# A four-part graph network on one core: another order of ScalarE's stages in the fourth gated pass, and a last part with four row buffers

## The chip, the cores and the metric

The kernel runs on one core of a Trainium2 chip. The metric is the device time of one execution in microseconds (us). The engines are TensorE (PE; its weight loads are PEld), VectorE (DVE), ScalarE (ACT), GpSimd (POOL) and SyncE (SP); an engine name with a q, as ACTq, is its queue of instructions that are not computation.

## The reference, cut to what matters

12,500 nodes with 64 features, 200,000 edges sorted by destination. Four networks follow each other, each with a layer norm and a relu ahead and its result added to `x`:

```
h = relu(layernorm(x)); x += GIN(h)            # sum over edges of relu(h[src]), then a two-layer MLP
h = relu(layernorm(x)); x += gated(h)          # 4 steps: message by edge type, sum over edges, GRU cell
h = relu(layernorm(x)); x += gcn(h)            # 2 convolutions: degree-normalised sum over edges
h = relu(layernorm(x)); x += edge_network(h)

GRU cell:  r, z = sigmoid(...);  n = tanh(i_n + r * h_n);  feat = (1 - z) * n + z * feat
edge net:  h = [x_dst, x_src - x_dst] @ W.T + b          # per edge
           h = (h - mean(h)) / sqrt(var(h) + eps) * gamma + beta    # over all edges
           h = where(h >= 0, h, 0.3 * h)
           result = segment_sum(h, dst) / max(counts, 1)
```

## The kernel before, in words

Edges lie in 1563 rows of 128 edges, nodes in 98 blocks of 128. A pass over the edges handles 1660 visits of (row, block) in 166 groups of ten, two groups to a span, 83 spans. There are eight passes: GIN, three gated ones, `MIXED` (the fourth gated pass with the first work of the convolutions), `CONV`, `LAST` and `EDGE`. In a pass:

- POOL gathers every row's 128 source nodes from a table in DRAM (line 476), one indirect DMA for a row, into a ring `RINGF` of 300 rows. For row 300 and on it waits until SP has told it (`ring_free`, L367) that PE is done with the rows that are overwritten. It can't begin a pass before the table of that pass is whole: SP counts the writes of the table (`sent`) and then raises `table_ready`.
- DVE writes one-hot matrices `OH` from the destinations (L1027), PE multiplies them with the gathered rows (L683) into PSUM, after two matmuls of zeros that clear the places (L679), and DVE adds the places to the sums in `A` (L1052).
- The node work runs beside this in steps called positions, 132 to a pass (`SLOTS`), each on a chunk of two blocks. The function `positions` emits, for each engine, the stages (lag, stage) in the order written: at position p a stage with lag k works on chunk number p - k. The first 83 positions go with the spans; the other 49 follow when all groups are summed. A table of chunks by position is worked out at run time; where no chunk is complete yet, a position works on a spare one, and so the passes always run all 132. A pass's table is whole in the first few positions behind the spans; the rest are spare ones, and PE and DVE begin the next pass only behind them.

In `MIXED` a chunk goes through these stages: DVE `pick` (L1084, lag 0), PE turns it, ACT `copied` (L540, 0), PE `gates`, ACT `gates` = Sigmoid (L570, 1), DVE `pre` (L1130, L1133, 1), ACT `bent` = Tanh (L576, 1), DVE `mix_last` (L1140 to L1166, 2) with `centre` (L1094, L1096), ACT `root` = two Squares with sums (L561) and a Sqrt (L564), lag 3, DVE `scaled` (reciprocal L1103, L1112, 3), PE `turn2` (L733), ACT `copied2` (L548, 3), PE, DVE `convolved` (L1177, L1178, 4), ACT `send` (L596, 4), which writes the table. ACT also fetches `XIN` for the chunk (L583). Sqrt is in another activation table than Sigmoid and Tanh, and the compiler puts an `ACT_TABLE_LOAD` ahead of each change.

The last part follows the `EDGE` pass, in which the rows before the norm were written to `kept` in DRAM; the one-hot matrices lie in DRAM as bf16 (`shorts`). For each of 166 groups: SP loads the rows (`LOADED`, two buffers, L430) and the one-hots (`OH16`, four buffers, L404, which waits for the product four groups back); DVE subtracts a middle (L1339) and takes max(0.3 t, t) (L1344, `ACTED`, four buffers); POOL splits that in two steps (`split` L507, `low` L502, one group later) into three bf16 parts; PE clears ten places (`zero`, L679) and runs 30 matmuls (L683); DVE adds them to the sums (L1331, `edge_add` of the group four back, between L1339 and L1344). `groups_in_fours` emits groups 0 to 5 and then a loop of four groups. Behind the loop, DVE writes a weight for each node and feature (L1349), multiplies and adds in two halves (L1359, L1360), and SP writes each half out (L437).

Of the kernel before, what the change touches and what calls it, by code (L numbers as in the profile page):

```python
# [13 lines left out]
P = 128  # L14
# [54 lines left out]
def gnn_kernel(nc, x, dst_rows, src_cols, type_cols, row_ends, batch_ends, L0_W1, L0_b1, L0_W2, L0_b2, L1_Wt, L1_b,  # L69
# [15 lines left out]
    with ExitStack() as ctx:  # L85
# [107 lines left out]
        LOADED, MOVED = (cut(RINGF, k * 2 * GRP * D, [2, GRP, D]) for k in range(2))  # L193
        ACTED, REST = (cut(RINGF, (1 + k) * 4 * GRP * D, [HOLD, GRP, D]) for k in range(2))
# [7 lines left out]
        def bank(k):  # L202
# [46 lines left out]
        kept_out, kept_in, drow_in = (sems(f"{n}0", f"{n}1") for n in ("kept_out", "kept_in", "drow_in"))  # L249
        short_out, short_in = sems("short_out0", "short_out1"), sems(*(f"short_in{k}" for k in range(HOLD)))  # L250
# [6 lines left out]
            sem(f"e_{n}") for n in ("moved", "acted", "rest", "low", "product", "added"))  # L257
        result, stored = sems("result", "stored")
# [66 lines left out]
        def _(sp):  # L325
# [90 lines left out]
            for h in range(2):  # L416
                sp.wait_ge(kept_out[h], 16)
                sp.dma_start(LOADED[:, h, :, :], kept[:, h * GRP:(h + 1) * GRP, :]).then_inc(kept_in[h], 16)
            for h in range(2):
                sp.wait_ge(kept_out[h], SPAN * 16)  # L420
            sp.wait_ge(e_counted, GROUPS)
# [17 lines left out]
            sp.wait_ge(stored, 32)  # L439
# [76 lines left out]
        def _(act):  # L516
# [40 lines left out]
            def root(turn):  # L557
# [840 lines left out]
```

## Time and profile before

| what | value |
|---|---|
| median of 3 runs | 16602.79 us (16602.6 to 16603.92) |
| the profiled execution, its own time | 16601.05 us |
| its span in the trace | 16599.2 us |
| granted PE clock, mean | 0.523 |
| busy: PE, PEld | 67%, 54% |
| busy: DVE, ACT, POOL | 34%, 14%, 74% |

Times in the trace count from the start of the span. A row of the timeline gives start and duration in us, the engine, the line of the kernel, the operation, what it writes <- reads, how many are merged, and in brackets how long the engine sat idle before it and what ended that. POOL's busy time is the issue of its gathers. "issue" is time in which the engine waited for nothing that the profile shows. POOL holds the largest share of the chain that ended last; the order in which engines are busy says where in the 16.6 ms other engines hold it up.

### The profile page before, as it was taken

The numbers are of one execution on the slowest core, as the hardware profiler recorded it, in microseconds if no ns is written. First come the engines' busy times: TensorE is split into PE (matmuls) and PEld (weight loads), VectorE is DVE, ScalarE is ACT, GpSimd is POOL, SyncE is SP. The second block draws the span as 40 slices with busy tenths as digits, with TensorE's granted clock in tenths as the row PEclk, the third lists the DMA queues.
The fourth block names the chain that finished last, engine by engine and source line by source line (L and its number), as shares of the span: only waits on it lengthen the run. The fifth ranks groups of instructions, "written<-read, shape, count | busy, mean of one in ns | idle before, by whom it ended". The sixth has DMA issues, their size and how long they took to land.

```text
span 16599.2 us, 246663 instructions
## 1 busy us (share of the span) xinstructions
PE 11186.9 (67%) x47842; PEld 8971.1 (54%) x47843; DVE 5583.8 (34%) x12782; ACT 2283.6 (14%) x5885; POOL 12248.7 (74%) x12861
## 2 busy tenths in 40 slices
PE   4666787767776677766776665666565555787776
PEld 3455555555555555555565553455454444687765
DVE  3222333323332243322443333322232223422247
ACT  1111130001100020000222224211100000100000
POOL 6777677776777767777677776677777777777776
PEclk5555555556655565555755555555555555555555
DMA  2111121112211121111211111222211111333345
GB/s 53 40 40 41 43 67 40 39 38 50 51 39 38 38 61 40 39 38 38 62 33 32 32 32 36 57 66 65 59 39 32 32 32 34 86 93 83 83 136 191
DMA packets 727921, 891.48 MB, mean 54 GB/s; under 512 B 251262, under 2 KB 352847, under 8 KB 727200
## 3 DMA queue, kind: packets, MB, share of 16 engines
q0 software_dynamic: 400544, 411.38, 14.2%
q1 hardware_dynamic: 113184, 233.19, 4.4%
q10 hardware_dynamic: 213984, 244.81, 4.2%
q14 instruction: 161, 1.32, 0.0%
q8 instruction: 48, 0.79, 0.0%
HBM read 590.99 MB, written 297.44 MB: 54 GB/s over the span
## 4 chain that ended last, share of the span: by engine, by line
POOL 51%; issue 23%; DMA 14%; PE 6%; DVE 2%; DVEq 1%; SPq 1%; ACT 0%; ACTq 0%; POOLq 0%
POOL RINGF L476 51%; DMA RINGF<-tab_gated,IDX 7%; PE ps L683 4%; DMA RINGF<-tab_gcn,IDX 4%; DMA RINGF<-tab_gin,IDX 2%; DMA RINGF<-tab_edge,IDX 1%; PE ps L679 1%; DVEq L1067 1%; SPq L365 1%; PE ps L777 0%; DVE TEMP L1084 0%; DVE ps L1140 0%; DVE TEMP L1142 0%; PE ps L716 0%; DVE TEMP L1130 0%
## 5 line engine op out<-in xcount | busy, mean ns | idle before, releaser
L476 POOL DMA_INDIRECT RINGF<-tab_gated,IDX x6252 | 5903.9, 944 | 2044.5 <-issue 1775.8
L683 PEld LDWEIGHTS ps<-RINGF,OH 128*128 128x128 f32 (+1 forms) x28220 | 5316.4, 296 | 1739.6 <-issue 1739.6
L683 PE MATMUL ps<-RINGF,OH 128*128 (+1 forms) x28220 | 5560.3, 392 | 1026.3 <-SPq L362 1022.0
L476 POOL DMA_INDIRECT RINGF<-tab_gcn,IDX x3126 | 2951.0, 944 | 1098.5 <-issue 943.4
L1052 DVE TENSOR_TENSOR A<-A,ps 128x640 f32 x1162 | 954.4, 821 | 7886.6 <-PE ps L683 7886.6
L679 PE MATMUL ps<-ZERO 1*128 1x325 bf16 x2656 | 927.8, 451 | 2460.7 <-issue 2454.1
L476 POOL DMA_INDIRECT RINGF<-tab_gin,IDX x1563 | 1483.4, 949 | 504.0 <-issue 444.0
L476 POOL DMA_INDIRECT RINGF<-tab_edge,IDX x1563 | 1476.4, 945 | 506.5 <-issue 446.4
L1027 DVE TENSOR_TENSOR OH<-ps,DLOC 128x1280 f32<-128x1280 f32 x1162 | 1723.4, 1484 | 0.3
L679 PEld LDWEIGHTS ps<-ZERO 1*128 1x128 bf16 x2656 | 174.5, 99 | 2818.0 <-issue 2812.6
L733 PE MATMUL ps<-IDENT,TEMP 128*64 128x128 f32 x1848 | 535.9, 390 | 619.4 <-DVE TEMP L1112 202.7
L821 PE MATMUL ps<-IDX,OH 128*128 (+1 forms) x3320 | 727.6, 351 | 304.5 <-ACT OH L640 304.5
L764 PE MATMUL ps<-WG,TEMP 128*128 128x256 f32 x2112 | 902.4, 575 | 0.0
L777 PE MATMUL ps<-WT,TEMP 65*128 65x256 f32 x2112 | 887.0, 565 | 15.5 <-ACT TEMP L548 15.2
L821 PEld LDWEIGHTS ps<-IDX,OH 128*128 128x128 f32 x3320 | 724.7, 332 | 316.3 <-issue 316.3
L570 ACT ACTIVATE TEMP<-ps 128x256 f32<-128x256 f32 x528 | 201.1, 381 | 4865.5 <-PE ps L764 4864.7
L716 PE MATMUL ps<-IDENT,TEMP 128*128 128x128 f32 (+1 forms) x1320 | 387.1, 391 | 649.7 <-DVE TEMP L1084 608.8
L548 ACT ACTIVATE TEMP<-ps 64x256 f32<-64x256 f32 x924 | 346.3, 375 | 3378.0 <-PE ps L733 3039.9
L811 PE MATMUL ps<-A,TEMP 128*128 x3320 | 748.1, 423 | 8.0 <-DVE TEMP L1252 8.0
L716 PEld LDWEIGHTS ps<-IDENT,TEMP 128*128 128x128 f32 (+1 forms) x1320 | 167.3, 177 | 1066.3 <-issue 1064.0
L811 PEld LDWEIGHTS ps<-A,TEMP 128*128 128x128 f32 x3320 | 728.0, 333 | 8.9 <-issue 8.9
L764 PEld LDWEIGHTS ps<-WG,TEMP 128*128 128x128 f32 x2112 | 633.2, 300 | 118.9
(206 smaller groups left out, 7972.5 us busy)
## 6 DMA issues: line engine op xcount, KB each, us to landing
tab_gated<-TEMP ACTq DMA_DIRECT2D x528, 256.0 KB
RINGF<-tab_gated,IDX POOLq DMA_INDIRECT x6252
shorts<-TEMP ACTq DMA_DIRECT2D x166, 320.0 KB
TEMP<-dloc_dram SPq DMA_DIRECT2D x166, 320.0 KB
kept<-OH SPq DMA_DIRECT2D x166, 320.0 KB
RINGF<-kept SPq DMA_DIRECT2D x166, 320.0 KB, 3.3
OH<-shorts SPq DMA_DIRECT2D x166, 320.0 KB, 3.0
RINGF<-tab_gcn,IDX POOLq DMA_INDIRECT x3126
```

What stands on the lines that cost most here:

```text
L476: nc.gpsimd.indirect_dma_start(out=RINGF[:, at:at + D], out_offset=None, in_=table, in_offset=bass.IndirectOffsetOnAxis(ap=index[:, k:k + ...
L548: nc.scalar.activation(XT[0:D, odd, :], ps_t2[0:D, :], func).then_inc(s_copied2, 1)
L679: nc.tensor.matmul(ps[:, base + k * BANK:base + k * BANK + HALF * PITCH], ZERO[:, 0:P], ZERO[:, 0:HALF * PITCH], start=True, stop=True)
L683: return nc.tensor.matmul(ps[:, base:][:, bass.ds(place, width)], onehots_, rows_, start=False, stop=False, skip_group_check=True)
L716: ins = nc.tensor.transpose(ps_t[0:width, k * P:(k + 1) * P], PICK[:, odd, k, 0:width], IDENT[:, :])
L733: ins = nc.tensor.transpose(ps_t2[0:D, k * P:(k + 1) * P], NEXT[:, odd, k, :], IDENT[:, :])
L764: ins = nc.tensor.matmul(ps_gate[odd][:, k, :], XG[:, odd, k * P:(k + 1) * P], WG[:, :], start=False, stop=False, skip_group_check=True)
L777: ins = nc.tensor.matmul(out_[:, k, :], XT[0:rows, odd, k * P:(k + 1) * P], weights, start=True, stop=True)
L811: ins = nc.tensor.matmul(ps_u[:, h, u // HALF, u % HALF, :], OTS[:, h, u, :], Af[:, D:][:, bass.ds(at[u], D)], start=True, stop=True)
L821: ins = nc.tensor.matmul(ps_stat[w][:, bass.ds(2 * g, 2)], table[:, h, u:u + 2, :].rearrange("p u f -> p (u f)"), MASK[:, bass.ds(g * GRP ...
L1027: return V.tensor_tensor(OH[:, h, :, :], ps_ramp[h].unsqueeze(1).broadcast_to([P, GRP, P]), cols.unsqueeze(2).broadcast_to([P, GRP, P]), A ...
L1052: ins = V.tensor_tensor(into, into, ps_g[:, h, :, :, 0:D], ALU.add)
```

## The change: what it does

In `MIXED`, ACT's stage `root` is cut in two, `spread` (the Squares) and `root` (the Sqrt). They ran first in a position, at lag three; now `spread` stands behind `copied` and `root` behind `bent`, both at lag two. On DVE `scaled` now comes ahead of `pick`. In GIN and `LAST` the two halves follow each other as before.

In the last part `LOADED` has four buffers in place of two (`MOVED`, with two, lies elsewhere), four groups are loaded ahead, and SP issues a row load when the group four back has been moved. ACT writes the zeros of each group's places into PSUM, from the constant `NONE`, when the group two back has been added, and PE's two matmuls of zeros are gone: PE waits for ACT's zeros in their place. ACT also writes the weights, one instruction for each of 98 blocks, between the zeros; DVE's one instruction for them is gone. The result is finished and written in four pieces of 42, 32, 18 and 6 blocks.

```diff
--- before.py
+++ after.py
@@
+PIECES = [(0, 42), (42, 74), (74, 92), (92, 98)]
@@
-        LOADED, MOVED = (cut(RINGF, k * 2 * GRP * D, [2, GRP, D]) for k in range(2))
-        ACTED, REST = (cut(RINGF, (1 + k) * 4 * GRP * D, [HOLD, GRP, D]) for k in range(2))
+        LOADED, ACTED, REST = (cut(RINGF, k * HOLD * GRP * D, [HOLD, GRP, D]) for k in range(3))
+        MOVED = cut(RINGF, 14 * GRP * D + NB * D, [2, GRP, D])
@@ block.sync
-            for h in range(2):
-                sp.wait_ge(kept_out[h], 16)
-                sp.dma_start(LOADED[:, h, :, :], kept[:, h * GRP:(h + 1) * GRP, :]).then_inc(kept_in[h], 16)
+            def load_back(g, k):
+                sp.dma_start(LOADED[:, k, :, :], kept[:, bass.ds(g * GRP, GRP), :]).then_inc(kept_in[k], 16)
+
+            def load_group(g, h, k, i, q):
+                if later(g, HOLD):
+                    sp.wait_ge(e_moved, g - HOLD + 1)
+                    load_back(g, k)
+                    sp.wait_ge(e_product, g - HOLD + 1)
+                    load_short(g, k)
+
+            for g in range(HOLD):
+                sp.wait_ge(kept_out[g % 2], (g // 2 + 1) * 16)
+                load_back(g, g)
...
-            def load_group(g, h, k, i, q):
-                if later(g, 2):
-                    sp.wait_ge(e_moved, g - 1)
-                    sp.dma_start(LOADED[:, h, :, :], kept[:, bass.ds(g * GRP, GRP), :]).then_inc(kept_in[h], 16)
-                if later(g, HOLD):
-                    sp.wait_ge(e_product, g - HOLD + 1)
-                    load_short(g, k)
             groups_in_fours(load_group)(sp)
-            for k in range(2):
+            for k, (first, last) in enumerate(PIECES):
                 sp.wait_ge(result, k + 1)
-                sp.dma_start(out[:, k * NB // 2:(k + 1) * NB // 2, :], X3[:, k * NB // 2:(k + 1) * NB // 2, :]
-                             ).then_inc(stored, 16)
+                sp.dma_start(out[:, first:last, :], X3[:, first:last, :]).then_inc(stored, 16)
@@ block.scalar
-            def root(turn):
+            def spread(turn):
                 def stage(s, odd, i, tail):
                     act.wait_ge(s_cen, turn * SLOTS + s + 1)
                     for k in range(CH):
                         nc.scalar.activation(SQ[:, k, :], CEN[:, odd, k, :], ACT.Square, scale=0.125,
                                              accum_out=LN[:, odd, 1, k:k + 1]).then_inc(s_sq, 1)
+                return stage
+
+            def root(turn):
+                def stage(s, odd, i, tail):
                     act.wait_ge(s_sq, (turn * SLOTS + s + 1) * CH)
@@ block.scalar, the mixed pass
-            positions(act, no_groups, (3, root(1)), (1, gates(MIXED)), (0, copied(MIXED, P)),
-                      (1, bent(MIXED)), (3, copied2(MIXED, ACT.Copy)), (0, fetch),
+            positions(act, no_groups, (1, gates(MIXED)), (0, copied(MIXED, P)), (2, spread(1)),
+                      (1, bent(MIXED)), (2, root(1)), (3, copied2(MIXED, ACT.Copy)), (0, fetch),
                       (4, send(MIXED, tab_gcn[0], D, s_conv, 0)))
@@ block.scalar, the last part
+            act.wait_ge(e_moved, 1)
+
+            def weigh(b):
+                nc.scalar.activation(A3[:, bass.ds(b, 1), D:P], ST[:, S_SCALE:S_SCALE + 1, :], ACT.Copy,
+                                     scale=CNT[:, bass.ds(b, 1)]).then_inc(e_weighed, 1)
+
+            def zero_places(g, h, k, i, q):
+                if later(g, 2):
+                    act.wait_ge(e_added, g)
+                nc.scalar.activation(places[:, h, :, 0:HALF * PITCH], NONE[:, :, 0:1].broadcast_to([P, 2, HALF * PITCH]),
+                                     ACT.Copy).then_inc(e_zeroed, 1)
+                if isinstance(g, int):
+                    for b in range(3 * g, 3 * g + 3):
+                        weigh(b)
+                elif h == 0:
+                    weigh(i + 15)
+            groups_in_fours(zero_places)(act)
@@ block.tensor, sum_group
-                if later(g, 2):
-                    pe.wait_ge(e_added, g)
-                    pe.sem_inc(pe_go, 1)
-                zero(base)
+                pe.wait_ge(e_zeroed, g + 1)
+                pe.sem_inc(pe_go, 1)
                 pe.wait_ge(e_low, g + 1)
@@ block.vector, the mixed pass
-            positions(dve, sum_edges(MIXED), (0, pick(MIXED, False)), (3, scaled(MIXED, 1, False)), (2, mix_last),
+            positions(dve, sum_edges(MIXED), (3, scaled(MIXED, 1, False)), (0, pick(MIXED, False)), (2, mix_last),
                       (1, pre(MIXED)), (4, convolved(MIXED, 0, 4)))
@@ block.vector, sum_step and after it
-                    dve.wait_ge(kept_in[h], i * 16 + 16)
-                    V.tensor_tensor(MOVED[:, h, :, :], LOADED[:, h, :, :], middle, ALU.subtract).then_inc(e_moved, 1)
+                    dve.wait_ge(kept_in[k], q * 16 + 16)
+                    V.tensor_tensor(MOVED[:, h, :, :], LOADED[:, k, :, :], middle, ALU.subtract).then_inc(e_moved, 1)
...
-            link(V.tensor_tensor(FEAT, ST[:, S_SCALE:S_SCALE + 1, :].broadcast_to([P, NB, D]), over_f(CNT), ALU.mult))
...
+            dve.sem_inc(dve_go, 1)
+            dve.wait_ge(e_weighed, NB)
-            for k in range(2):
-                half = slice(k * NB // 2, (k + 1) * NB // 2)
+            for first, last in PIECES:
+                part = slice(first, last)
```

ACT's instructions in one position of `MIXED` behind the spans, before (L561 Squares, L564 Sqrt, L570 Sigmoid, L540 `copied`, L576 Tanh, L548 `copied2`):

```order
L561 ACTIVATE TEMP<-TEMP 128x64 x2
L564 ACT_TABLE_LOAD
L564 ACTIVATE TEMP<-TEMP,EPSC 128x2
L570 ACT_TABLE_LOAD
L570 ACTIVATE TEMP<-ps 128x256
L540 COPY TEMP<-ps 128x256
L576 ACTIVATE ps<-TEMP 128x2x64
L548 ACTIVATE TEMP<-ps 64x256
```

And now (L579 Sigmoid, L545 `copied`, L566 Squares, L585 Tanh, L573 Sqrt, L553 `copied2`):

```order
L579 ACT_TABLE_LOAD
L579 ACTIVATE TEMP<-ps 128x256
L545 COPY TEMP<-ps 128x256
L566 ACTIVATE TEMP<-TEMP 128x64 x2
L585 ACTIVATE ps<-TEMP 128x2x64
L573 ACT_TABLE_LOAD
L573 ACTIVATE TEMP<-TEMP,EPSC 128x2
L553 ACTIVATE TEMP<-ps 64x256
```

The Squares and the Sqrt with its table load moved from the head of the position to both sides of the Tanh; there are two table loads in either. DVE's instructions at the head of such a position, before (L1084 `pick`, L1103 and L1112 `scaled`, L1140 the first of `mix_last`; L1067 reads a chunk's number):

```order
L1084 COPY TEMP<-A 128x256
L1103 RECIPROCAL TEMP<-TEMP 128x2
L1112 SCALAR_TENSOR_TENSOR TEMP<-TEMP 128x128
L1067 ISA
L1067 TENSOR_LOAD LISTS
L1067 ISA x2
L1140 ISA
L1140 TENSOR_TENSOR ps<-A,ps 128x2x64
```

And now (L1127 and L1136 `scaled`, L1108 `pick`, L1091 reads the chunk's number; `mix_last` follows):

```order
L1127 RECIPROCAL TEMP<-TEMP 128x2
L1136 SCALAR_TENSOR_TENSOR TEMP<-TEMP 128x128
L1091 ISA
L1091 TENSOR_LOAD LISTS
L1091 ISA x2
L1103 REGISTER_ALU
L1105 REGISTER_ALU
L1108 ISA
L1108 COPY TEMP<-A 128x256
```

`pick`, with the reading of its chunk number, moved from ahead of the reciprocal to a place behind `scaled`. PE's instructions in the last part's loop, from the last reading of the places to a group's first matmuls, before:

```order
L671 TENSOR_LOAD LISTS
L847 ISA
L679 MATMUL ps<-ZERO 128x325 x2
L853 REGISTER_ALU
L683 ISA
L683 MATMUL ps<-RINGF,OH 128x64 x3
```

And now:

```order
L697 ISA
L697 TENSOR_LOAD LISTS
L875 REGISTER_ALU
L709 ISA
L709 MATMUL ps<-RINGF,OH 128x64 x3
```

The two matmuls of zeros left, and nothing came in their place but a wait.

## Rows read from the trace of the kernel before

**Rows 1.** The page, part 4: the chain that ended last, by engine.

```profile
POOL 51%; issue 23%; DMA 14%; PE 6%; DVE 2%; DVEq 1%; SPq 1%; ACT 0%; ACTq 0%; POOLq 0%
```

**Rows 2.** Timeline of POOL: start, duration (us), engine, line, operation [idle before].

```profile
10039.54 0.94 POOL L476 DMA_INDIRECT RINGF<-tab_gcn,IDX  x1 [65.45 <-issue]
...
10476.97 0.94 POOL L476 DMA_INDIRECT RINGF<-tab_gcn,IDX  x1 [62.21 <-SPq L367]
```

**Rows 3.** Timeline of ACT and DVE, one position after the mixed pass's last group.

```profile
10206.74 0.29 ACT L564 ACTIVATE TEMP<-TEMP,EPSC 128x2 f32<-128x2 f32 x1
10207.05 1.28 ACT L570 ACT_TABLE_LOAD   x1
10207.06 0.17 DVE L1103 RECIPROCAL TEMP<-TEMP 128x2 f32<-128x2 f32 x1 [2.39 <-ACT TEMP L564]
...
10211.31 0.29 DVE L1133 TENSOR_TENSOR TEMP<-TEMP,ps 128x128 f32<-128x128 f32 x1
10211.63 0.28 ACT L576 ACTIVATE ps<-TEMP 128x128 f32<-128x128 f32 x1 [2.63 <-DVE TEMP L1133]
10211.84 0.36 ACT L548 ACTIVATE TEMP<-ps 64x256 f32<-64x256 f32 x1
...
10213.82 0.29 DVE L1084 COPY TEMP<-A 128x256 f32 x1 [0.75 <-issue]
...
10214.85 1.28 ACT L564 ACT_TABLE_LOAD   x1
```

**Rows 4.** Line L564 in two stretches (min/median/max ns, first and last start); timeline.

```profile
L564 ACT ACTIVATE TEMP<-TEMP,EPSC x21: 295/296/296, 8403.8 to 8789.7; 128x2 f32<-128x2 f32 x21
...
L564 ACT ACTIVATE TEMP<-TEMP,EPSC x52: 295/295/296, 9992.3 to 10464.1; 128x2 f32<-128x2 f32 x52
...
10036.15 0.36 ACTq L596 DMA_DIRECT2D tab_gcn<-TEMP  x1
...
10440.06 0.29 ACT L564 ACTIVATE TEMP<-TEMP,EPSC 128x2 f32<-128x2 f32 x1
...
10470.86 1.27 ACT L628 ACTIVATE TEMP<-OH 128x1280 bf16<-128x1280 f32 x1 [4.22 <-DVE OH L1027]
```

**Rows 5.** Chain in order of time, last part: start, us, what.

```profile
16300.92 0.70 PE ps L679 x2
16301.62 1.71 PE ps L683 x30
```

**Rows 6.** Timeline of POOL and DVE in the last part's loop.

```profile
16038.67 1.25 POOL L507 TENSOR_TENSOR RINGF<-RINGF 128x640 f32<-128x640 f32 x1
...
16041.68 1.25 POOL L507 TENSOR_TENSOR RINGF<-RINGF 128x640 f32<-128x640 f32 x1
...
16300.23 1.25 POOL L507 TENSOR_TENSOR RINGF<-RINGF 128x640 f32<-128x640 f32 x1 [0.76 <-DVE RINGF L1344]
...
16301.43 1.25 POOL L502 TENSOR_TENSOR RINGF<-RINGF 128x640 bf16<-128x640 f32 x1
...
16302.31 1.06 DVE L1344 SCALAR_TENSOR_TENSOR RINGF<-RINGF 128x640 f32<-128x640 f32 x1
16303.45 1.25 POOL L507 TENSOR_TENSOR RINGF<-RINGF 128x640 f32<-128x640 f32 x1 [0.76 <-DVE RINGF L1344]
...
16304.15 0.82 DVE L1339 TENSOR_TENSOR RINGF<-RINGF,ps 128x640 f32<-128x640 f32 x1 [0.79 <-DMA RINGF<-kept]
```

**Rows 7.** Timeline of the end; last row: the page's part 6.

```profile
16566.47 1.25 POOL L507 TENSOR_TENSOR RINGF<-RINGF 128x640 f32<-128x640 f32 x1 [0.76 <-DVE RINGF L1344]
...
16570.49 6.68 DVE L1349 TENSOR_TENSOR A<-ST,CNT 128x6272 f32<-128x6272 f32 x1
...
16578.07 1.78 DVE L1331 TENSOR_TENSOR A<-A,ps 128x640 f32 x2 [0.90 <-DVE A L1349]
...
16590.25 3.42 DVE L1360 TENSOR_TENSOR RINGF<-RINGF,A 128x3136 f32<-128x3136 f32 x1
...
RINGF<-kept SPq DMA_DIRECT2D x166, 320.0 KB, 3.3
```

More of the change, by code:

```diff
@@ L59 @@
 TINY = 1e-20
+PIECES = [(0, 42), (42, 74), (74, 92), (92, 98)]
 FAR = 1 << 20
 assert (GROUPS - 6) % HOLD == 0
+assert PIECES[-1][1] == NB == 3 * 6 + 2 * ((GROUPS - 6) // HOLD)
 assert GROUPS * GRP == VISITS and 2 * SPAN == GROUPS and SPAN % 2 == 1 and SLOTS % 2 == 0
@@ L247, in gnn_kernel @@
         x3_in, x_held = sems("x3_in", "x_held")
-        kept_out, kept_in, drow_in = (sems(f"{n}0", f"{n}1") for n in ("kept_out", "kept_in", "drow_in"))
-        short_out, short_in = sems("short_out0", "short_out1"), sems(*(f"short_in{k}" for k in range(HOLD)))
+        kept_out, short_out, drow_in = (sems(f"{n}0", f"{n}1") for n in ("kept_out", "short_out", "drow_in"))
+        kept_in, short_in = (sems(*(f"{n}{k}" for k in range(HOLD))) for n in ("kept_in", "short_in"))
         short_set = sem("short_set")
@@ L257, in gnn_kernel @@
             sem(f"e_{n}") for n in ("moved", "acted", "rest", "low", "product", "added"))
+        e_zeroed, e_weighed = sems("e_zeroed", "e_weighed")
         result, stored = sems("result", "stored")
@@ L414, in _ @@
                 keep(GROUPS - 2 + h, h)
-            for h in range(2):
-                sp.wait_ge(kept_out[h], 16)
-                sp.dma_start(LOADED[:, h, :, :], kept[:, h * GRP:(h + 1) * GRP, :]).then_inc(kept_in[h], 16)
+            def load_back(g, k):
[9 more added lines that the diff above has]
+                load_back(g, g)
+            sp.wait_ge(e_counted, GROUPS)
             for h in range(2):
                 sp.wait_ge(kept_out[h], SPAN * 16)
-            sp.wait_ge(e_counted, GROUPS)
             for g in range(HOLD):
@@ L609, in _ @@
             positions(act, no_groups, (1, hidden), (0, copied(GIN, D)), (4, typed(GIN)),
-                      (4, send(GIN, tab_gated[1], TYPES * D, s_typed, GIN)), (3, copied2(GIN, ACT.Copy)), (2, root(0)),
-                      (2, store(x_gin, 0)))
+                      (4, send(GIN, tab_gated[1], TYPES * D, s_typed, GIN)), (3, copied2(GIN, ACT.Copy)), (2, spread(0)),
+                      (2, root(0)), (2, store(x_gin, 0)))
             act.wait_ge(sums, SUMS_AT[1])
@@ L633, in _ @@
             positions(act, shorten, (0, copied2(CONV, ACT.Relu)), (1, send(CONV, tab_gcn[1], D, s_conv, 1)))
-            positions(act, no_groups, (1, copied2(LAST, ACT.Copy)), (0, root(2)), (0, store(x_last, 2)),
+            positions(act, no_groups, (1, copied2(LAST, ACT.Copy)), (0, spread(2)), (0, root(2)), (0, store(x_last, 2)),
                       (2, send(LAST, tab_edge, D, s_conv, 2)))
@@ L1356, in _ @@
             dve.wait_ge(x3_in, 16)
-            for k in range(2):
-                half = slice(k * NB // 2, (k + 1) * NB // 2)
-                link(V.tensor_tensor(SUMS[:, half, :], SUMS[:, half, :], FEAT[:, half, :], ALU.mult))
-                V.tensor_tensor(X3[:, half, :], X3[:, half, :], SUMS[:, half, :], ALU.add).then_inc(result, 1)
+            dve.sem_inc(dve_go, 1)
+            dve.wait_ge(e_weighed, NB)
+            for first, last in PIECES:
+                part = slice(first, last)
+                link(V.tensor_tensor(SUMS[:, part, :], SUMS[:, part, :], FEAT[:, part, :], ALU.mult))
+                V.tensor_tensor(X3[:, part, :], X3[:, part, :], SUMS[:, part, :], ALU.add).then_inc(result, 1)
 def kernel(**inputs):
```

2 lines of the change are left out of this document (1 added, 1 removed).

## The prediction

> **What bounds the kernel now.** I first read the chain that ended last [rows 1]. POOL leads it with 51%, and the next share, "issue", is mostly the handover between its gathers: over the whole program POOL is the pacer, and another engine costs time only where POOL stands still or where there is no gathering. So I went through POOL's timeline for its long pauses. Between the fourth gated pass and the first convolution there are two [rows 2]: 65.45 us before the first gather of `CONV`, in which the table must become whole, and 62.21 us before its 301st. That the second one is released by SP's L367 (`ring_free`) says that the ring was full: PE had not begun `CONV`. It couldn't, since it was still in the spare positions of `MIXED`. The 300 gathers before it took 10414.76 - 10039.54 = 375.2 us (10414.76 is where the pause began), 1.25 us each.
>
> Next, one such position in the timeline of ACT and DVE [rows 3]. It is a circle. The Sqrt ends at 10207.03 and lets DVE's reciprocal go, which had waited 2.39; DVE runs through `scaled`, `mix_last` and `pre` and ends L1133 at 10211.60; the Tanh had waited for it for 2.63; then ACT has `copied2`, the two DMAs, the Squares, a table load from 10214.85 and the next Sqrt. Each engine waits once for the other. From 9992.3 to 10440.06 that makes 48 positions [rows 4], 9.33 us each.
>
> Last I read the last part, where nothing is gathered. Its chain in order of time is PE alone: 0.70 of zeros, 1.71 of products [rows 5], and the reading of the next places. POOL's L507 starts at 16041.68 for group 5 and at 16566.47 for group 165 [rows 6, 7]: 3.28 us per group.
>
> **The circle in `MIXED`.** Now the Sqrt follows the Tanh directly, so the DMAs and the Squares no longer lie on the way from DVE's `pre` to the Sqrt. Counted from a Sqrt's end: DVE's old stretch to the end of L1133, 10211.60 - 10207.03 = 4.57; `pick` now lies in it, 0.75 of idle before it and 0.29 itself [rows 3], 1.04; Tanh 0.28, table load 1.28, Sqrt 0.29, handovers 0.07. Sum 7.53 us. The same way of counting gives for before 4.57 + 0.03 + 3.22 (Tanh's start to the load's) + 1.28 + 0.31 = 9.41 against the 9.33 measured, so it errs by under 0.1. Neither engine's own work is longer: ACT's is 9.33 - 2.63 = 6.7 us, DVE's from the reciprocal at 10207.06 to the end of `pick` at 10214.11 is 7.05. PE's matmuls for a position lie beside the circle. The Squares wait for `centre`, behind which DVE still has a copy and `pre`'s two operations of 0.29 [rows 3]; two Squares of 64 elements lie beside those. I take 7.53, 1.80 less per position; the bounds are DVE's 7.05 and the old 9.33.
>
> What that gives. (1) The last chunk that the table needs is picked in the first position behind the spans and sent four positions later, by the DMA at 10036.15 [rows 4]. That is 4 x 1.80 = 7.2 less; but its `pick` now stands behind `scaled`, which costs about 1.1 once. 6.1 us. (2) From POOL's first `CONV` gather to the release of its ring it took 437.4 us, with 44 positions in them: 44 x 1.80 = 79 less is 358, and POOL needs 375 to fill the ring. The pause goes whole, 62.2 - 0.3 = 61.9 us. It would come back if a position took over 7.92. What is late next is POOL's own issue of gathers. Both together: 68.0 us. While the spans run, a longer or shorter position costs nothing: POOL covers it (see the slower rival). The other passes have the same instructions as before.
>
> **The last part's loop.** Taking the zeros from PE shortens its 3.28 by at least 0.6, to 2.7 or less. So PE is out, and I ask who is next. The rows on POOL and DVE [rows 6] show it: L1344, which has the same size as L1339 (0.82 us), took 1.06 when it began at 16302.31, while L502 ran until 16302.68, and POOL's next L507 started only when it was done, after 0.76 of idle. So the three work in turn: L507 1.21 to L502's start, L502 1.25, then 0.76, together 3.22 us for a group (16300.23 to 16303.45). That turn has no PE and no DMA in it. I take 3.22: 160 groups x 0.06 = 9.6 us. The row loads had DVE wait 0.79 before L1339 once here; SP still issues each behind the one-hot load that waits for PE's product, so the four buffers alone don't start it earlier, but PE's earlier product does, and with its wait gone DVE still meets POOL's L502 on the way. Below, the bound is groups 4 and 5, 16038.67 to 16041.68, 3.01 us, when DVE was ahead and L1344 slipped in between POOL's two; above, the old 3.28.
>
> By the Trainium skill (SBUF — State Buffer, "SBUF: two separate sides") VectorE with two SBUF inputs and GpSimd share one port pair by an exclusive lock that is held for the whole instruction. This case's rows agree: 1.06 in place of 0.82 where they overlap. Without such a lock the loop would fall to DVE's three operations of 0.82 and their handovers, about 2.85, and the part would gain 70 us more or less; with it hardly anything is left for the two matmuls to give.
>
> ScalarE's write of zeros, 2 x 325 per partition into PSUM, isn't in the trace. Nearest rows: Tanh with 128 into PSUM, 0.28 [rows 3]; a copy of 1280, 1.27 [rows 4]. I take 0.8, between them by size. It starts when DVE has added the group two back, and that add ends before L1344, so even at 1.27 the zeros are there about 0.7 us after POOL's `low`; a product of 1.7 that starts that much later still ends a group ahead of its add. It costs nothing at either end. The 98 weights of 64 elements each (0.28 or less) go where ACT waits for DVE.
>
> **The end.** Before, POOL's last L507 began at 16566.47 and DVE's last add ended at 16579.85 [rows 7], 13.4 us: PE was two groups behind, and DVE's 6.68 us for the weights stood in the way. Now: L507 and two L502 3.7, of which the last product waits; PE takes 1.71 for each product and 3.28 - 0.70 - 1.71 = 0.87 between them, so two products from the first L502's end (2.6 after L507's start) end at 6.9; add 1.1. That is 8.0, 5.4 less. The final four operations become eight: same elements, 4 x 0.16 of fixed cost more (6.68 against 2 x 3.42 gives 0.16), 0.6 us. Behind the last one at 16593.67 lay 5.5 us until the span's end, for a half of 1568 KB; the last piece has 192 KB, and 320 KB land in 3.3 [rows 7]; with the third piece's rest I take 3.5. 2.0 - 0.6 = 1.4 us.
>
> **Sum.** 6.1 + 61.9 + 9.6 + 5.4 + 1.4 = 84.4 us. The profiled execution took 16601.05 (span 16599.2), so 16516.7 in its frame; the median of the runs is 1.7 above it, so 16518.4.
>
> **Rivals.**
> A. The loop finds the faster turn of 3.01 and keeps it: 160 x 0.21 = 34 us more, 16485. For: there are no waits on row loads at first. Against: a row load must be issued two groups after the product that lets SP go on, and it takes 3.3 us; before, the faster turn held for four groups only.
> B. A switch of tables costs more behind the Tanh than the load's 1.28. If ACT first had to run empty, for about as long as one more load, a position would take 8.81, 0.52 less in place of 1.80: 1.0 us ahead of the table, 23 of the pause. With the last part 40 us, 16562. Against: the load at 10207.05 starts 0.02 after the end of the Sqrt ahead of it [rows 3], so nothing is paid there. The Trainium skill (ScalarE: Activation LUTs, "What ACT_TABLE_LOAD costs") has such a drain, ~1380 ns, with each switch, by which the sum would be 16567; the row agrees with its 1283 ns for the load and shows no drain.
> C. The pause is only handed on: POOL fills the ring at once, but DVE and PE in `CONV`, which also wait for ACT's shortening of the one-hots (1.27 each), can't follow, and the 62 us come back at the pass's end: 16580. Against: PE starts `CONV` with fewer rows waiting than before, when the ring was full, and POOL made no third long pause.
> D. Slower. The stages of a position in `MIXED` also run between PE's groups. PE takes its queue in order: `turn` waits for `pick`, which now waits behind `scaled` for the previous position's Sqrt. If that stretches a span over POOL's 1563 x 1.25 / 83 = 23.5 us, each microsecond costs 83. At 25 us: 124 lost against 84 won, 16643. Against: when PE was catching up, positions followed each other every 19.3 us [rows 4], and `scaled`'s Sqrt is then a whole span old. It decides from 24.6 us.
>
> **How the numbers follow.** The forecast 0.73, A 0.10, B 0.06, C 0.06, D 0.05. The forecast's own range is 16495 (a position of 7.05 and half of A) to 16545 (a position of 8.4: 21 us of the pause stay, and 3.5 ahead of the table). A change within 0.2%, 33 us, counts as none; a measurement of this kernel tells hardly less. A and B are faster by more than that; C lies within; D is slower: 0.89, 0.06, 0.05. The range of 8 in 10 takes in A and goes up to the forecast's end and a part of B: 16482 to 16558.
>
> **What would show it.** In the changed kernel's trace: no pause of POOL before the 301st gather of `CONV`, and about 59 us before its first; the Sqrt every 7.5 us behind `MIXED`'s spans, with the load 0.02 behind the Tanh; in the last part L507 every 3.2 us, with 0.76 of idle after L1344, L1344 over 0.82, no L679; the weights' instruction gone; less than 9 us from the last L507 to the last add. A pause at the 301st gather, or a position over 7.92, would make the large term wrong; L507 every 3.0 us would be A; positions over 23.5 us apart in the spans, D.

## The result, and the profile after

The changed kernel takes 16527.74 us (median of 6 runs, 16527.18 to 16529.08), beside 16602.53 for the kernel before (6 runs, 16600.69 to 16603.92). That is 74.8 us less, a ratio of 0.9955 with a 95% interval of 0.9942 to 0.9968. 16518.4 had been forecast, 84.4 less. Sign and range hold, and so does the large term in `MIXED`. The term for the last part's loop does not. On one of the chips used for the experiments most runs had each pass some 4 us longer (the kernel before: 16633 in place of 16602), so each experiment is compared with the kernel before on its own chip, and by stretches of the trace.

The time by stages, from POOL's gathers in both traces (us):

| stretch | before | after | forecast |
|---|---|---|---|
| last gather of `MIXED` to first of `CONV` | 65.45 | 59.16 | 59.35 |
| first gather of `CONV` to its last | 2013.68 | 1951.54 | 1951.8 |
| last gather of all to the span's end | 592.76 | 587.15 | 576.4 |
| everything else (two spans less the above) | 13927.3 | 13927.5 | as before |

The chain that ended last, by engine (the page, part 4), answers to [rows 1]:

```profile
POOL 58%; issue 23%; DMA 15%; PE 1%; DVE 1%; SPq 1%; DVEq 0%; POOLq 0%; ACTq 0%; ACT 0%
```

PE's share fell from 6% to 1% and POOL's rose by 7 points. That is no gain of 5% of the span: the chain in the last part merely runs over POOL now where it ran over PE, and the next rows show how little that part's time changed. What a chain names is whose work it passed through, not what would be saved.

POOL's timeline at `CONV`'s beginning, answering to [rows 2]:

```profile
10033.05 0.94 POOL L481 DMA_INDIRECT RINGF<-tab_gcn,IDX  x1 [59.16 <-issue]
...
10449.54 0.94 POOL L481 DMA_INDIRECT RINGF<-tab_gcn,IDX  x1 [0.90 <-issue]
```

The pause of 62.21 is gone. The only idle time over 0.6 us that POOL has left in `CONV` is 0.90 before the 334th gather.

One position behind `MIXED`'s spans, in the timeline of ACT and DVE, answering to [rows 3]:

```profile
10199.67 0.29 DVE L1157 TENSOR_TENSOR TEMP<-TEMP,ps 128x128 f32<-128x128 f32 x1
10199.99 0.28 ACT L585 ACTIVATE ps<-TEMP 128x128 f32<-128x128 f32 x1 [0.30 <-DVE TEMP L1157]
10200.29 1.28 ACT L573 ACT_TABLE_LOAD   x1
...
10201.59 0.29 ACT L573 ACTIVATE TEMP<-TEMP,EPSC 128x2 f32<-128x2 f32 x1
...
10201.91 0.17 DVE L1127 RECIPROCAL TEMP<-TEMP 128x2 f32<-128x2 f32 x1 [0.48 <-ACT TEMP L573]
...
10203.54 0.45 DVE L1108 COPY TEMP<-A 128x256 f32 x1 [0.91 <-issue]
...
10207.36 0.28 ACT L585 ACTIVATE ps<-TEMP 128x128 f32<-128x128 f32 x1 [0.30 <-DVE TEMP L1157]
```

The Tanh, the table load 0.02 behind its end, the Sqrt 0.02 behind the load: nothing is paid for a drain. DVE's wait for the Sqrt fell from 2.39 to 0.48, the Tanh's wait for DVE from 2.63 to 0.30. The line's own summary for the stretch, answering to [rows 4]:

```profile
L573 ACT ACTIVATE TEMP<-TEMP,EPSC x52: 295/295/296, 9991.5 to 10369.5; 128x2 f32<-128x2 f32 x52
```

51 steps in 378.0 us are 7.41 us for each, where [rows 4] give (10464.1 - 9992.3) / 51 = 9.25.

The last loop turn of the last part, PE, POOL, DVE and ACT, answering to [rows 5, 6]; the number in brackets is the idle time ahead:

```profile
16485.82 1.78 PE L709 MATMUL ps<-RINGF,OH 128*128 128x64 bf16 x30 [1.28 <-issue]
...
16489.07 1.82 PE L709 MATMUL ps<-RINGF,OH 128*128 128x64 bf16 x30 [1.47 <-issue]
...
16492.15 1.78 PE L709 MATMUL ps<-RINGF,OH 128*128 128x64 bf16 x30 [1.25 <-issue]
...
16494.42 1.25 POOL L512 TENSOR_TENSOR RINGF<-RINGF 128x640 f32<-128x640 f32 x1 [0.76 <-DVE RINGF L1368]
16494.85 0.82 DVE L1363 TENSOR_TENSOR RINGF<-RINGF,ps 128x640 f32<-128x640 f32 x1 [0.51 <-DMA RINGF<-kept]
...
16495.81 1.79 PE L709 MATMUL ps<-RINGF,OH 128*128 128x64 bf16 x30 [1.89 <-issue]
...
16496.73 0.71 ACT L668 ACTIVATE ps<-NONE 128x650 f32<-128x650 f32 x1 [2.23 <-DVE A L1355]
...
16498.94 1.81 PE L709 MATMUL ps<-RINGF,OH 128*128 128x64 bf16 x30 [1.33 <-issue]
```

PE has 1.8 of products for each group and stands idle for the rest, but the releaser is "issue": no other engine holds it. Four starts on are 16498.94 - 16485.82 = 13.12 us, 3.28 each, exactly what a group took before. What PE's own queue does in such a gap is in the trace too (`--source L697`, the reading of the ten places, from 16496.9 to 16498.9):

```profile
L697 PEldq TENSOR_LOAD <-LISTS x3: 327/332/334, 16497.1 to 16498.1; - x3
```

Three reads of 0.33 us, half a microsecond apart. The first starts when the products of the group before still run, the last ends at 16498.4, and behind it come the group's waits and register operations until its first product at 16498.94. Ahead of the reads the queue has a register operation for each of the ten places, spread over the products. So it is at work from one group's first product to the next one's.

The end, answering to [rows 7]:

```profile
16497.64 1.25 POOL L512 TENSOR_TENSOR RINGF<-RINGF 128x640 f32<-128x640 f32 x1 [0.76 <-DVE RINGF L1368]
...
16505.32 1.80 PE L709 MATMUL ps<-RINGF,OH 128*128 128x64 bf16 x30 [1.32 <-issue]
16507.38 0.82 DVE L1355 TENSOR_TENSOR A<-A,ps 128x640 f32 x1 [2.30 <-PE ps L709]
16508.46 2.96 DVE L1384 TENSOR_TENSOR A<-A 128x2688 f32<-128x2688 f32 x1 [0.26 <-DVE A L1355]
...
16514.44 8.59 SPq L443 DMA_DIRECT2D out<-RINGF  x4
...
16522.10 0.56 DVE L1385 TENSOR_TENSOR RINGF<-RINGF,A 128x384 f32<-128x384 f32 x1
```

POOL's last `split` to the last add's end: 10.56 us (13.38 before). From there to the span's end: 17.1 (19.3 before).

### The profile page after: what moved, and what is told of

Same layout as the page of the kernel before. It is cut to its first block, busy times and chain, and to the rows that moved or that the text cites. A ratio compares the mean times of both kernels' runs of the same rounds, so it can differ in the third digit from the quotient of the medians.

```text
span 16525.3 us, 246610 instructions
## 1 busy us (share of the span) xinstructions
PE 11107.3 (67%) x47510; PEld 8984.8 (54%) x47511; DVE 5602.7 (34%) x12785; ACT 2430.0 (15%) x6149; POOL 12247.7 (74%) x12861
## 3 DMA queue, kind: packets, MB, share of 16 engines
q14 instruction: 162, 1.33, 0.0%
## 4 chain that ended last, share of the span: by engine, by line
POOL 58%; issue 23%; DMA 15%; PE 1%; DVE 1%; SPq 1%; DVEq 0%; POOLq 0%; ACTq 0%; ACT 0%
POOL RINGF L481 56%; DMA RINGF<-tab_gated,IDX 8%; DMA RINGF<-tab_gcn,IDX 4%; DMA RINGF<-tab_gin,IDX 2%; DMA RINGF<-tab_edge,IDX 2%; POOL RINGF L507 1%; PE ps L709 1%; POOL RINGF L512 1%; SPq L368 0%; DVEq L1091 0%; PE ps L803 0%; DMA tab_gin<-A 0%; POOLq L472 0%; PE ps L705 0%; PE ps L742 0%
## 5 line engine op out<-in xcount | busy, mean ns | idle before, releaser
L705 PE MATMUL ps<-ZERO 1*128 1x325 bf16 x2324 | 811.6, 450 | 2313.6 <-issue 2308.2
L579 ACT ACTIVATE TEMP<-ps 128x256 f32<-128x256 f32 x528 | 201.0, 381 | 4970.7 <-PE ps L790 4969.6
L803 PE MATMUL ps<-WT,TEMP 65*128 65x256 f32 x2112 | 920.2, 583 | 15.4 <-ACT TEMP L553 15.3
L553 ACT ACTIVATE TEMP<-ps 64x256 f32<-64x256 f32 x924 | 346.2, 375 | 3403.2 <-PE ps L759 3064.1
```

Source lines behind the costliest of these rows:

```text
L553: nc.scalar.activation(XT[0:D, odd, :], ps_t2[0:D, :], func).then_inc(s_copied2, 1)
L705: nc.tensor.matmul(ps[:, base + k * BANK:base + k * BANK + HALF * PITCH], ZERO[:, 0:P], ZERO[:, 0:HALF * PITCH], start=True, stop=True)
L803: ins = nc.tensor.matmul(out_[:, k, :], XT[0:rows, odd, k * P:(k + 1) * P], weights, start=True, stop=True)
```

## The experiments

Three questions: which part of the change brought what; why the last part's loop kept its 3.28; what would shorten it. All edits are to the changed kernel. "Last part" is from POOL's last gather to the span's end, and a group's time is from POOL's split for the sixth group to the last one, over 160.

**1. The last part's edits alone.** `MIXED` in the order of before.

```
-  positions(act, ..., (1, gates(MIXED)), (0, copied(MIXED, P)), (2, spread(1)), (1, bent(MIXED)), (2, root(1)), ...
+  positions(act, ..., (3, spread(1)), (3, root(1)), (1, gates(MIXED)), (0, copied(MIXED, P)), (1, bent(MIXED)), ...
-  positions(dve, ..., (3, scaled(MIXED, 1, False)), (0, pick(MIXED, False)), (2, mix_last), ...
+  positions(dve, ..., (0, pick(MIXED, False)), (3, scaled(MIXED, 1, False)), (2, mix_last), ...
```

> Only the last part is changed; ScalarE's and VectorE's order in the mixed pass is that of before. By the two traces the last part gave 5.6 us (592.8 to 587.2 us from POOL's last gather to the end), so the main theory (two separate effects that add) expects 16597 us, a ratio of 0.9997, with POOL's pause of 62 us at the 301st gather of CONV there again. Rival: the pause and the last part are coupled by the state in which the passes run; then it is below 16590 us.

Measured: 16602.28 us beside 16607.65 for the kernel before on the same chip, ratio 0.9997 (0.9987 to 1.0007). The pause is back:

```profile
10477.48 0.94 POOL L481 DMA_INDIRECT RINGF<-tab_gcn,IDX  x1 [62.56 <-SPq L370]
```

The last part takes 587.66, as with the whole change (587.15), beside 592.76. So all that the last part's edits bring is 5.1 us by the traces and 5.4 by the medians, whose interval doesn't exclude nothing at all; `MIXED`'s orders bring the rest.

**2. ACT's new order alone**, DVE's `pick` ahead of `scaled` as before.

```
-  positions(dve, ..., (3, scaled(MIXED, 1, False)), (0, pick(MIXED, False)), (2, mix_last), ...
+  positions(dve, ..., (0, pick(MIXED, False)), (3, scaled(MIXED, 1, False)), (2, mix_last), ...
```

> The changed kernel, but VectorE keeps its old order, pick ahead of scaled; ScalarE's new order stays. Theory 'circle': pick then lies outside the way from Sqrt to Tanh, where it is short by 7.4 - 1.04 = 6.3 us, and a position is bound by VectorE's own 7.05 us or ScalarE's 6.7: Sqrts 7.0 to 7.2 us apart behind the spans, no pause at the 301st gather, the gap before CONV's first gather 57 us in place of 59.2, the time 1 to 3 us below the changed kernel's 16527.7. Rival 'VectorE's swap is needed': with pick first, the reciprocal comes late and positions stay near 9 us, so that 30 to 60 us of the pause come back.

Measured: 16527.31 us, 80.3 less than before on that chip (the whole change: 74.8 on its own), ratio 0.9952 (0.9935 to 0.9968). The line of the Sqrt, and POOL's first gather of `CONV`:

```profile
L573 ACT ACTIVATE TEMP<-TEMP,EPSC x52: 295/295/296, 9993.1 to 10340.2; 128x2 f32<-128x2 f32 x52
```

```profile
10030.72 0.94 POOL L481 DMA_INDIRECT RINGF<-tab_gcn,IDX  x1 [52.93 <-issue]
```

A position takes 347.1 / 51 = 6.81 us and the gap 52.93, 6.2 less than with both orders; 57 had been expected, and 7.0 to 7.2 for a position. DVE's half of the change is a loss. With both orders the first `pick` behind the spans, at 9993.28, stands 19.4 us behind `MIXED`'s last gather, since it has to wait for `scaled`; here, as in the kernel before, it stands 15.5 behind it. That is 3.9 once. The four positions behind it take 2.9 less, since `pick` no longer lies between the Sqrt and the next Tanh, and 0.6 are lost from the fourth `pick` after it to the last send.

**3. DVE's new order alone**, ACT's as before.

```
-  positions(act, ..., (1, gates(MIXED)), (0, copied(MIXED, P)), (2, spread(1)), (1, bent(MIXED)), (2, root(1)), ...
+  positions(act, ..., (3, spread(1)), (3, root(1)), (1, gates(MIXED)), (0, copied(MIXED, P)), (1, bent(MIXED)), ...
```

> The changed kernel, but ScalarE keeps its old order in the mixed pass (Squares and Sqrt first, lag three), and VectorE has the new one, pick behind scaled. Theory 'circle': pick is added to a way that was 9.33 us long, so 10.4 us for a position, the pause at the 301st gather 62 + 44 x 1.04 = 108 us, the gap before CONV about 70 us, in all 16597 + 51 = 16648 us. Rival 'VectorE's order alone gives part of the gain': the position is below 9.33 us and the time below 16597.

Measured: 16657.34 us (one run), 50 more than the kernel before.

```profile
10537.40 0.94 POOL L481 DMA_INDIRECT RINGF<-tab_gcn,IDX  x1 [115.69 <-SPq L370]
```

The gap ahead of `CONV` is 73.21, a position (10524.5 - 9993.8) / 51 = 10.41. The circle that the forecast drew, with one link longer, gives a longer pause: the same mechanism with the other sign.

**4. The zeros back on PE**, none by ACT.

```
-                if later(g, 2):
-                    act.wait_ge(e_added, g)
-                nc.scalar.activation(places[:, h, :, 0:HALF * PITCH], NONE[:, :, 0:1].broadcast_to([P, 2, HALF * PITCH]),
-                                     ACT.Copy).then_inc(e_zeroed, 1)
...
-                pe.wait_ge(e_zeroed, g + 1)
-                pe.sem_inc(pe_go, 1)
+                if later(g, 2):
+                    pe.wait_ge(e_added, g)
+                    pe.sem_inc(pe_go, 1)
+                zero(base)
```

> The changed kernel with PE's two matmuls of zeros back in the last part's loop, and none of ScalarE's zeros. Theory 'PE's instruction stream' (the time between two groups' products is that in which PE's queue reads the ten places into registers, and the zeros lay beside it): the loop stays at 3.27 us per group and the time within 2 us of 16527.7. Theory of the prediction (0.6 us per group on PE, then the port's turn): the loop goes up by 0.06, 10 us, to 16538.

Measured: last part 587.57, 3.279 a group; 16534.13 us, ratio 0.9956 (0.9939 to 0.9972). By the time alone neither expectation is met, but it is 73.5 under the kernel before on the same chip, where the change is 74.8 under it, and the trace has its longer time outside the last part: the last row of the table of stretches is 13932.5 here and 13932.2 in experiment 2 on the same chip, beside 13927.5. In the last part the two matmuls that the change takes away cost nothing. PE's timeline shows why:

```profile
16498.00 0.70 PE L701 MATMUL ps<-ZERO 1*128 1x325 bf16 x2 [0.66 <-issue]
16498.63 1.78 PE L705 MATMUL ps<-RINGF,OH 128*128 128x64 bf16 x30
...
16501.67 0.70 PE L701 MATMUL ps<-ZERO 1*128 1x325 bf16 x2 [1.26 <-issue]
16502.30 1.79 PE L705 MATMUL ps<-RINGF,OH 128*128 128x64 bf16 x30
...
16505.41 1.81 PE L705 MATMUL ps<-RINGF,OH 128*128 128x64 bf16 x30
```

Products start at 16498.63, 16502.30 and 16505.41, 3.67 and 3.11 apart; without the zeros they start 3.66 and 3.13 apart. The 0.66 of idle and 0.63 of zeros have become 1.33 of idle. In the queue the zeros stand behind the three reads and ahead of the register operations for the products, so those went on while the array had the zeros: in the kernel before the next reads start 0.86 us behind a group's first product (16301.55 and 16302.41), in the changed kernel 1.25 (16495.81 and 16497.06). From the last split to the last add it takes 10.50 us here, as with the change, so the end's gain doesn't come from the zeros either.

**5. PE doesn't read the places**, but writes each chunk to a fixed one (this leaves the last network's sums out of their right places).

```
-                at = load_many(LOC, g, BANK + (HALF - 1) * PITCH)
-                        ins = accumulate(base, at[u], D, OH16[:, k, u, :], part)
+                        to = base + u // HALF * BANK + u % HALF * PITCH
+                        ins = nc.tensor.matmul(ps[:, to:to + D], OH16[:, k, u, :], part, start=False, stop=False, ...)
```

> The changed kernel, but in the last part's loop PE doesn't read the ten places of a group from the table: every group adds to the same ten fixed places, which leaves the sums of the last network wrong; instructions of other engines are the same. Theory 'PE's instruction stream': PE needs under 2.7 us per group and waits for others; POOL and VectorE are then the pace, 3.22 us per group or less, 8 us off the loop, 16520. Rival 'row loads': the loop is set by VectorE's wait for its rows, which follow PE's product through SP; it stays at 3.26 us per group, 16527.

Measured: 16516.72 us (one run), last part 575.33, 3.223 a group, last split to last add 7.02.

```profile
16303.09 1.80 PE L880 MATMUL ps<-RINGF,OH 128*128 128x64 bf16 x30 [1.42 <-POOL RINGF L507]
...
16303.79 1.25 POOL L512 TENSOR_TENSOR RINGF<-RINGF 128x640 f32<-128x640 f32 x1 [0.76 <-DVE RINGF L1369]
```

PE now waits for POOL's L507, and the group takes what the forecast said of the turn of POOL and DVE, 3.22. The edit takes two things out of PE's queue, the three reads and the register operation for each place, so it is the two together that held the loop at 3.28; which has what share wasn't tried apart.

**6. Row loads one step earlier**: SP issues each ahead of the one-hot load that waits for PE.

```
-                    sp.wait_ge(e_product, g - HOLD + 1)
-                    load_short(g, k)
+                if later(g, HOLD + 1):
+                    sp.wait_ge(e_product, g - HOLD)
+                    load_short(g - 1, (k + 3) % HOLD)
...
+            sp.wait_ge(e_product, GROUPS - HOLD)
+            load_short(GROUPS - 1, (GROUPS - 1) % HOLD)
```

> The changed kernel; SP issues the row load of a group one step earlier, ahead of the one-hot load of the group before. Theory 'PE's instruction stream': VectorE's waits for rows (78.7 us in all) go, and it waits for PE's product instead; the loop stays at 3.26 us, the time within 2 us of 16527.7. Rival 'row loads': the loop falls to the port's turn of 3.22 us or to 3.0, 7 to 40 us less.

Measured: 16527.71 us, ratio 0.9955 (0.9938 to 0.9972); 3.269 a group, last part 587.26. Nothing gained: the 78.7 us in which the changed kernel's L1363 waits for its rows are gone, and DVE stands idle ahead of its adds for 144.3 us instead of 38.1, all but 0.1 of it for PE's products. The rows are no bound of this loop.

**7. PE's loop with eight groups in its body**, so half as many branches.

```
+                with eng.Fori(0, (GROUPS - 6) // (2 * HOLD)) as j:
+                    for r in range(2 * HOLD):
+                        body(2 * HOLD * j + 6 + r, r % 2, (6 + r) % HOLD, 4 * j + 3 + r // 2,
+                             2 * j + (6 + r) // HOLD)
-            groups_in_fours(sum_group)(pe)
+            groups_in_eights(sum_group)(pe)
```

> The changed kernel; PE's loop over the groups of the last part has eight groups to a turn in place of four, so the branch (a gap of 1.9 instead of 1.3 us once per turn) comes half as often. Theory 'PE's instruction stream': 0.6 / 8 = 0.07 us per group less, until the port's turn of 3.22 binds: 6 to 8 us, 16521. Rival 'row loads': no change.

Measured: 16517.93 us (16517.2 to 16519.63), ratio 0.9949 (0.9933 to 0.9966); 3.223 a group, last part 577.35.

```profile
16300.19 1.78 PE L719 MATMUL ps<-RINGF,OH 128*128 128x64 bf16 x30 [1.47 <-issue]
...
16303.02 1.25 POOL L522 TENSOR_TENSOR RINGF<-RINGF 128x640 f32<-128x640 f32 x1 [0.76 <-DVE RINGF L1378]
16303.32 1.82 PE L719 MATMUL ps<-RINGF,OH 128*128 128x64 bf16 x30 [1.35 <-issue]
...
16304.60 1.56 DVE L1378 SCALAR_TENSOR_TENSOR RINGF<-RINGF 128x640 f32<-128x640 f32 x1
...
16306.25 1.25 POOL L522 TENSOR_TENSOR RINGF<-RINGF 128x640 f32<-128x640 f32 x1 [0.76 <-DVE RINGF L1378]
```

In fours PE's products are 3.25, 3.08 and 3.13 apart inside the body and 3.66 over the branch (the rows of the changed kernel), (3.25 + 3.08 + 3.13 + 3.66) / 4 = 3.28, more than the turn's 3.22: PE sets the pace, and POOL's splits are unevenly apart, from 3.22 to 3.64, 45 of the last 159 over 3.24. With eights the same queue needs (7 x 3.15 + 3.66) / 8 = 3.21, just under the turn, and POOL's splits are 3.22 or 3.23 apart, all 152 from 16000 us on: the turn sets the pace.

**8. The edits of 6 and 7 together.**

> Both edits, eight groups to PE's loop and row loads a step earlier. Theory 'PE's instruction stream': 3.19 to 3.22 us per group, 7 to 12 us less than the changed kernel, 16518. Rival 'row loads': the same as with the row loads alone.

Measured: 16516.43 us, ratio 0.9948 (0.9931 to 0.9965); 3.213 a group, last part 576.92, 0.4 less than with the eights alone.

**9. The edits of 5 and 6 together** (the same part left out as in 5).

> Fixed places on PE (the sums of the last network are wrong by it) and row loads a step earlier, both in the changed kernel. With fixed places alone the loop was 3.223 us per group. Theory 'two turns': with rows there in time and PE out of the way, VectorE stays ahead and its L1368 goes between GpSimd's two operations, 3.01 us per group as in the first groups, 34 us below fixed places alone, about 16483. Rival 'one turn': the port's order of 3.22 us holds whatever is ahead, the time stays at 16517.

Measured: 16479.97 us (one run), last part 540.1, 3.005 a group.

```profile
16300.93 1.25 POOL L515 TENSOR_TENSOR RINGF<-RINGF 128x640 f32<-128x640 f32 x1
...
16301.24 1.62 DVE L1372 SCALAR_TENSOR_TENSOR RINGF<-RINGF 128x640 f32<-128x640 f32 x1
...
16302.14 1.83 POOL L510 TENSOR_TENSOR RINGF<-RINGF 128x640 bf16<-128x640 f32 x1
...
16303.93 1.25 POOL L515 TENSOR_TENSOR RINGF<-RINGF 128x640 f32<-128x640 f32 x1
```

POOL has no idle time any more: L1372 starts while L515 runs, ends 0.68 after it, and it is now POOL's L510 that takes 1.83. This is rival A's faster turn, and it holds for the whole loop. It wants both conditions, rows that are there and a PE below 3.0 a group; each alone gives 3.22 or more.

**10. The best of these: the edits of 2, 6 and 7.**

> The changed kernel with VectorE's old order in the mixed pass (pick first), PE's loop of eight groups, and row loads a step earlier. If the effects add: 6.2 us (gap before CONV 52.9 in place of 59.2) and 10.2 us: 16511. If they don't, 16517.

Measured: 16543.35 us beside 16633.49 on the same chip, ratio 0.9946 (0.9932 to 0.9959). By stretches: gap ahead of `CONV` 52.96 and last part 577.39, which is 6.2 and 9.8 less than the change. It is 90.1 us under the kernel before, where the change is 74.8 under it. By stretches and differences it is the best version, 15 to 16 us ahead of the change; the intervals of the two ratios overlap.

**11. The same with forty groups in PE's body.**

```
-            groups_in_eights(sum_group)(pe)
+            groups_in_forties(sum_group)(pe)
```

> The same with 40 groups to a turn of PE's loop. Theory 'PE's instruction stream' with a floor of 3.13 us per group and 0.6 us for each branch: 3.13 + 0.6 / 40 = 3.145 in place of 3.21, 10 us less than with eight, 16501. Rival: the longer code has to be fetched and costs as much, or the port's turn holds 3.2: no change against eight groups.

Measured: 16557.38 us, ratio 0.9954 (0.9940 to 0.9968); 3.293 a group, last part 591.44. The shorter group that was expected didn't come; this is 14.0 us more than with eight groups, by the medians and by the last part alike. POOL's splits are 3.22 apart but for three, at groups 50, 90 and 130, a body's length apart, where they are 6.78, 7.29 and 7.14 apart:

```profile
16107.65 1.25 POOL L525 TENSOR_TENSOR RINGF<-RINGF 128x640 f32<-128x640 f32 x1 [0.76 <-DVE RINGF L1381]
...
16110.76 1.78 PE L722 MATMUL ps<-RINGF,OH 128*128 128x64 bf16 x30 [5.78 <-POOL RINGF L520]
16112.79 0.82 DVE L1368 TENSOR_TENSOR A<-A,ps 128x640 f32 x1 [4.49 <-PE ps L722]
```

The wait is put down to POOL's L520, but in experiment 7's body of eight PE's waits for the same operation are 1.5 at most; here PE itself is late, and DVE and then POOL wait for it. PE's queue shows on what: the loop's branch. Its instruction in the changed kernel (`--source L308`) and here (`--source L318`), in ns:

```profile
L308 PEldq COMPARE_BRANCH  x38: 207/208/208, 16007.1 to 16493.4; - x38
...
L318 PEldq COMPARE_BRANCH  x3: 3847/3871/4073, 16104.4 to 16371.4; - x3
```

And the queue of instructions from 15962 to 16500 us (`--dma`), in the changed kernel, with eights (experiment 7) and here: packets, MB, share:

```profile
q8 instruction: 3, 0.05, 0.0%
...
q8 instruction: 4, 0.07, 0.1%
...
q8 instruction: 55, 0.90, 0.7%
```

With forty groups in the body the branch back to its beginning takes 3.6 to 3.9 us longer, and 55 packets of instructions are fetched in four turns, where the loops of four and eight groups need 3 and 4 in all. So the long body is fetched again in every turn. That the branch waits for this fetch is argued from these rows and not shown by itself; lengths between eight and forty weren't tried.

**12. The result in two pieces** in place of four.

```
-PIECES = [(0, 42), (42, 74), (74, 92), (92, 98)]
+PIECES = [(0, 49), (49, 98)]
```

> The changed kernel with the result written in two halves again. By the prediction's sizes the four pieces bring 1.4 us; by the trace after, from VectorE's last add to the span's end 17.1 us against 19.3 before, they bring 2.2. I expect 19.2 to 19.4 us there; if the weights' move had brought it, it would stay at 17.1.

Measured (one run, 16561.78 us, on the chip of 10): last add to the end 19.46 us beside 17.09. The pieces bring 2.4 us.

## Why the prediction was right or wrong

**The circle in `MIXED`: right.** The gap was forecast 6.1 shorter and is 6.3 shorter; the pause 61.9 and 62.1. A position was worked out as 7.53 and takes 7.41. In the gap the four positions behind the first `pick` take 30.37 us (`pick` at 9993.28 and 10023.65) where they took 37.54 (9989.60 and 10027.14): 7.17 less, 7.2 forecast. The 1.1 to be paid once is 0.9, the balance of a first `pick` that comes 3.9 later and of 3.0 less from the fourth `pick` behind it to the send. Experiments 2 and 3 move one link of the circle each: without `pick` in it the gap is shorter and no pause comes, with `pick` in the old circle the pause grows to 115.69. The forecast priced `pick` in its new place at 1.04 per position and 1.1 once, 5.3 in all; experiment 2 measures 6.2 in other parts, 3.9 once and 2.9 in four positions, less 0.6. So it saw the loss, but not that it could simply be left out.

**The loop: the failed step** is "Taking the zeros from PE shortens its 3.28 by at least 0.6, to 2.7 or less. So PE is out". It took the time of PE per group to be a sum: zeros, products, and the reading of the places. But the reads and the register operations belong to PE's queue of instructions and the zeros to its array, and the queue went on beside the zeros. Idle and zeros together were 0.66 + 0.63, and idle alone is 1.33 (experiment 4). So a group stayed at 3.28: 0.5 us won in place of 9.6. The next step, that POOL and DVE turn at 3.22, was right, and shows as soon as PE is really shortened (experiments 5 and 7). The trace before would have told: over the loop 127.9 of the 129.0 us of PE's gaps ahead of the zeros had "issue" as their releaser, its queue has the same three reads of 332 ns in each group, and the forecast called that gap "the reading of the next places" and then treated it as if it would stay at 0.87 whatever lay behind it.

**ACT's zeros: right.** 0.715 us against an assumed 0.8, and ACT waits for DVE before each (2.23 in the row above). They cost nothing here, and they bring nothing either.

**The end: the same step once more.** "PE takes 1.71 for each product and 3.28 - 0.70 - 1.71 = 0.87 between them" was to give 8.0 us from last split to last add. Their starts are 3.13 apart inside a body, so it takes 10.56. With fixed places it is 7.02. Half of the 5.4 came, 2.8, and the same came with the zeros back on PE (10.50, experiment 4); of the end's edits that leaves the weights' 6.68, which is off DVE's way as forecast, though no run moved it alone. The pieces bring 2.2 where 1.4 was forecast, 2.4 in experiment 12.

**Sum.** 6.3 + 62.1 + 0.5 + 2.8 + 2.2 = 73.9 of the two spans' difference, 16599.2 - 16525.3 = 73.9. Of the 10.5 missing from the forecast, 9.1 are the loop and 2.6 the end's products, less 1.2 from the other terms. By its own terms the lower end of the forecast's own range comes out at 16499.5 and not 16495 (17 for half of A, 4 x 0.48 for a position of 7.05), and the first L502's end lies 2.45 behind L507's start by [rows 6], not 2.6.

**The rivals.** A didn't come: 3.005 exists (experiment 9), but two things stand before it, and the forecast's reason against it, late rows, is one of them; alone it decides nothing (experiment 6). The other, PE at over 3.0 a group, is the failed step again. B: no drain, the load stands 0.02 behind the Tanh. C: the gap behind `CONV` is 18.81, it was 18.78, and POOL has no other pause in `CONV`. D: `MIXED`'s own gathers take 1952.56, before 1953.45; the spans weren't stretched.

## What to carry to other kernels

Where an engine's idle time reads "issue", look at what its own queue does in it (for PE the rows marked `PEldq` of `--source`). It need not be the queue: POOL's 59.16 ahead of `CONV` reads "issue" too. But where the queue is busy throughout, matmuls taken from between two such stretches don't shorten them: add up the queue, not the array. When a pacer waits for a circle of two engines, write the circle down link by link and move one link at a time; of two reorderings that came together, one brought everything and the other took 6 us back. A loop on one engine can be given a longer body than the others': eight groups in place of four brought 9.8 us, forty gave that back and 4.3 more.

## What was not expected of the hardware

- With ten places of each group read from a table into registers (three reads of 0.33 us) and used from there, PE's array has no products for 1.25 to 1.47 us a group, whether matmuls of 0.63 run in that time or not; at the loop's branch 1.89.
- A body of forty groups has PE stand for 5.78 us at its branch, where the body of four has 1.89: the branch instruction takes 3.85 to 4.07 us in place of 0.21.
- The three operations on shared rows have two steady patterns with the same instructions, 3.22 and 3.005 us a group. In the one POOL waits 0.76 for DVE; in the other POOL never waits, DVE's L1372 takes 1.62 (0.82 at the shortest) and POOL's L510 1.83 (1.25 otherwise). By the Trainium skill (SBUF — State Buffer, "SBUF: two separate sides") VectorE with two SBUF inputs and a GpSimd operation that reads SBUF never hold their shared port pair at once: the one that starts first keeps it for its whole instruction. The rows agree with that: L1372 ends 0.68 behind the L515 that it started beside, and L510, which started beside L1372, ends 1.11 behind it. In the faster pattern DVE's operation starts beside the split, in the slower one beside `low` (in experiment 5, L1369 beside L507, 1.84 us, and again it ends 0.68 behind it).
- ACT writes 650 zeros per partition into PSUM in 0.715 us.
